# Row halves of the array: the low half of an expansion and a 1x1 convolution on 48 partitions, for two units at a time

## What is computed

```python
# L0: channel attention, then three convolutions
q, k, v = split(norm(x) @ w_qkv + b_qkv)
q2 = l2n((q - mean)**2 / sum, axis=channels); k2 = l2n((k - mean)**2 / sum, axis=tokens)
attn = (v + q2 @ (k2.T @ v) / 64) @ w_ln + b_ln
y = leaky(conv1x1(concat(attn, x), w1) + b1)      # 96 -> 96: "conv1"
y = leaky(conv3x3(y, w2) + b2)                    # 96 -> 96: "conv2"
x = conv1x1(y, w3) + b3 + x
# L1: relu, depthwise 3x3, 1x1, norm
# L2: weights mixed from 4 experts by a gate on the mean of the image
h = relu(norm(x @ Wk))                            # 48 -> 192: "expansion"
h = relu(norm(depthwise3x3(h)))
x = norm(h @ Wk2) + x
# L3: as L1
```

## Time and profile before

| | |
|---|---|
| median of 3 runs | 1022.58 us |
| the profiled execution | 1021.38 us, its span 1019.5 us |
| TensorE (PE) | 961.8 us busy, 94% of the span |
| VectorE (DVE) | 861.8 us, 85% |
| ScalarE (ACT) | 483.4 us, 47% |
| GpSimd (POOL) | 78.2 us, 8% |
| mean granted TensorE clock | 0.98 of full speed |
| start of conv2 in iterations 3, 4, 5 | 388.7, 504.8, 620.8 us: 116.1 us each |

### The profile page before, as it was taken

The page is one execution under the profiler, slowest core; times in us unless marked ns, Lnnn a source line. Parts: engine busy times, 40 slices in busy tenths (PEclk is TensorE's granted clock), DMA queues, the critical chain, the costliest instruction groups (busy, mean ns, idle before and its releaser), DMA issues.

```text
span 1019.5 us, 15287 instructions
## 1 busy us (share of the span) xinstructions
PE 961.8 (94%) x4854; PEld 611.8 (60%) x4854; DVE 861.8 (85%) x1229; ACT 483.4 (47%) x827; POOL 78.2 (8%) x112
## 2 busy tenths in 40 slices
PE   4799989999999999999999999999999999997987
PEld 4455756566665675666665675666666576554624
DVE  5773689997899969998799969999699978997980
ACT  3311554264724655365724655355733746344532
POOL 0210021000300012000300002000300003000000
PEclk8799989999999999999999999999999999998999
DMA  5243733385517654186516655177425665145315
GB/s 79 49 125 73 132 83 98 61 141 124 137 47 120 129 126 122 33 134 155 131 48 106 134 122 140 27 126 163 114 72 91 131 130 139 38 93 127 63 34 104
DMA packets 129520, 104.49 MB, mean 102 GB/s; under 512 B 97903, under 2 KB 98772, under 8 KB 129492
## 3 DMA queue, kind: packets, MB, share of 16 engines
q1 hardware_dynamic: 122196, 102.76, 48.4%
q10 hardware_dynamic: 7296, 1.38, 1.0%
HBM read 10.82 MB, written 6.29 MB: 17 GB/s over the span
## 4 chain that ended last, share of the span: by engine, by line
PE 69%; DVE 15%; ACT 5%; SPq 5%; issue 4%; DMA 2%; ACTq 1%; DVEq 0%
PE bank L1329 27%; PE bank L1365 7%; PE bank L1309 5%; PE bank L1335 5%; DVE dwa L717 4%; PE bank L1433 3%; SPq L1031 3%; PE bank L1380 3%; PE bank L1349 3%; PE bank L1381 3%; PE bank L1299 2%; DVE dwa L733 2%; DMA y_parts<-a_parts 2%; PE bank L1368 2%; PE bank L1367 2%
## 5 line engine op out<-in xcount | busy, mean ns | idle before, releaser
L717 DVE SCALAR_TENSOR_TENSOR dwa<-h1a,dyn,dwa 128x1024 f32<-128x1024 f32 x224 | 279.9, 1274 | 3.7 <-ACT dwa L1615 3.0
L1329 PE MATMUL bank<-y_parts,w_l 128*96 128x512 f32 x576 | 149.6, 404 | 0.6 <-issue 0.3
L1329 PE MATMUL bank<-y_parts,w_h 128*96 128x512 f32 x576 | 147.6, 400 | 0.0
L717 DVE SCALAR_TENSOR_TENSOR dwb<-h1b,dyn,dwb 128x1024 f32<-128x1024 f32 x112 | 142.8, 1275 | 0.0
L1177 POOL TENSOR_TENSOR y_low<-y,y_parts 96x512 fp32r<-96x512 f32 x56 | 73.7, 1316 | 774.9 <-DVE y L771 774.9
L1329 PEld LDWEIGHTS bank<-y_parts,w_l 128*96 128x96 f32 x576 | 90.8, 162 | 61.5 <-issue 22.4
L1365 PE MATMUL bank<-a_parts,wt_h 128*112 128x512 f32 x384 | 116.3, 410 | 6.8 <-DMA y_parts<-a_parts 6.0
L1329 PEld LDWEIGHTS bank<-y_parts,w_h 128*96 128x96 f32 x576 | 92.9, 161 | 44.3
L1365 PEld LDWEIGHTS bank<-a_parts,wt_h 128*112 128x112 f32 x384 | 62.7, 174 | 42.8 <-issue 21.1
L1309 PE MATMUL bank<-xq,w_cur 97*96 97x512 f32 x128 | 67.9, 611 | 3.5 <-DVE y L771 3.5
L1650 ACT ACTIVATE y<-bank,b2s 96x512 f32<-96x512 f32 x32 | 21.9, 683 | 102.6 <-PE bank L1335 102.6
(11 more groups left out here) (265 smaller groups left out, 1621.9 us busy)
## 6 DMA issues: line engine op xcount, KB each, us to landing
y_parts<-y_parts SPq DMA_DIRECT2D x32, 396.0 KB, 3.5
y_parts<-a_parts SPq DMA_DIRECT2D x64, 198.0 KB, 3.0
y_parts<-a_parts SPq DMA_DIRECT2D x64, 197.6 KB, 3.5
y_parts<-y_low SPq DMA_DIRECT2D x64, 132.0 KB, 3.3
a_parts<-a_parts SPq DMA_DIRECT2D x128, 66.0 KB, 2.4
tok<-in_x_dram SPq DMA_DIRECT2D x42, 192.0 KB, 5.0
x_even<-y_parts SPq DMA_DIRECT2D x32, 198.0 KB, 3.6
x_odd<-y_parts SPq DMA_DIRECT2D x32, 198.0 KB, 4.0
```

Of the source, the lines that this page charges most:

```text
L717: nc.vector.scalar_tensor_tensor(out=dst, in0=tap_input(n, t), scalar=weight, in1=dst, op0=ALU.mult, op1=ALU.add).then_inc(tap_step, 1)
L1329: nc.tensor.matmul(bank[0:C2, :], wgt[:, t, :], y1_parts[:, part, rows, cols], start=part + t == 0, stop=False)
```

## The change

**Expansion.** `expand_pair(f, n)` does an even and an odd unit together. `x2[par]` now lies on 112 partitions with zeros between: for even rows the high part on 0 to 47 and the low part on 64 to 111, for odd rows the other way about. The weights are on both halves (`wpw`, `ew_h`, `ew_l` on 112 partitions). The high weights still multiply all of it; the low weights multiply the 48 partitions of the high part alone, which for even units are the upper half and for odd units the lower half of the array's rows. Both banks of `ring_b` are taken at the start of a pair.

**conv1.** The queries have a tile of their own, `q2`, with both parities side by side, so four transposes serve two units. `conv1_pair` multiplies the queries (`w1_q`, 48 rows) and x (`w1_x`, 49 rows with the one) in two matmuls for each unit, even on one row half and odd on the other; x is read from `xcm`, as `transpose_x` left it. The results go to banks 4 to 7 in turn, two at a time. The attention's small matmuls write their result for both halves.

**Loads.** `load_xt` reads both parities into `q2` (4 DMAs), `load_x` both into `tok` (4 DMAs): 8 for an image. `load_x` now stands after `beside_l1(2, 3)` on SP's queue.

```diff
-        expand_beside = {7: (), 8: (9, 10, 11), **{k: (k + 2,) for k in range(7)}}
+        expand_beside = ((2, 3), (4, 5), (6, 7), (8, 9), (10, 11))
...
             def conv1(image, f):
-                for k in range(CHUNKS + 1):
-                    if image is not None and k < CHUNKS:
-                        if k == 0:
+                for j in range(PCHUNKS + 1):
+                    units = expand_beside[j] if f is not None else ()
+                    if j < PCHUNKS:
+                        if j == 0:
                             pe.wait_ge(q_scaled, image + 1)
-                        par, i0 = k % 2, 4 * (k // 2)
-                        bank = ring_a.take(pe, image, A_XQ + k)
+                        bank = ring_a.take(pe, image, A_XQ + j)
                         for m in range(4):
-                            last = nc.tensor.transpose(bank[0:C2, m * 128:(m + 1) * 128],
-                                                       token(par, i0 + m, Q_AT, C2), ident[:, :])
+                            last = nc.tensor.transpose(bank[0:P2, m * 128:(m + 1) * 128], q2[:, 4 * j + m, :], ident[:, :])
                         last.then_inc(xqt_done, 1)
...
+                    if j < PCHUNKS:
+                        for n in units[:1]:
+                            expand_pair(f, n)
+                    if j > 0:
+                        conv1_pair(image, f, j - 1)
+                    if j == PCHUNKS:
+                        for n in units[:1]:
+                            expand_pair(f, n)
+
+            def conv1_pair(image, f, j):
+                if j == 0:
+                    pe.wait_ge(w1_ready, image + 1)
...
+                else:
+                    pe.wait_ge(y1_max, CHUNKS * image + 2 * (j - 1))
+                pe.wait_ge(xq_ready, PCHUNKS * image + j + 1)
+                pixels = slice(j * BANK, (j + 1) * BANK)
+                for par, at in enumerate((0, ODD_AT)):
+                    nc.tensor.matmul(conv1_bank(2 * j + par)[0:C2, :], w1_q[at:at + C, :], xq[at:at + C, j % 2, :],
+                                     start=True, stop=False)
+                for par, at in enumerate((0, ODD_AT)):
+                    nc.tensor.matmul(conv1_bank(2 * j + par)[0:C2, :], w1_x[at:at + C + 1, :], xcm[at:at + C + 1, pixels],
+                                     start=False, stop=True).then_inc(conv1_done, 1)
...
+            def expand_pair(image, n):
+                pair = [ring_b.take(pe, image, B_E + n + par) for par in range(2)]
+                g = (n if n < 4 else n - 4) // 2
+                parts = [(at, slice(r * ROWS, (r + 1) * ROWS))
+                         for at, r in (((E_OTHER, g), (E_BOTTOM, g + 2)) if n < 4 else ((0, g),))]
+                for nth, (at, rows) in enumerate(parts):
+                    for par in range(2):
+                        nc.tensor.matmul(pair[par][:, :], ew_h[:, at:at + M1], x2[par][:, rows, 1:W + 1], start=nth == 0, stop=False)
+                for nth, (at, rows) in enumerate(parts):
+                    for par in range(2):
+                        own = slice(par * ODD_AT, par * ODD_AT + C)
+                        last = nc.tensor.matmul(pair[par][:, :], ew_l[own, at:at + M1], x2[par][own, rows, 1:W + 1],
+                                                start=False, stop=nth == len(parts) - 1)
+                        if nth == len(parts) - 1:
+                            last.then_inc(expand_done, 1)
...
             def iteration(f, attn, back):
                 beside_l1(sp, f, (0, 1))
                 if attn is not None:
+                    load_xt(sp, attn)
+                beside_l1(sp, f, (2, 3))
+                if attn is not None:
                     load_x(sp, attn)
-                beside_l1(sp, f, (2, 3))
```

More of the change, by code:

```diff
@@ L1221, in _ @@
             nc.tensor.matmul(banks[5][0:SUMS, 0:C2], p1[:, :], w1a[:, :], start=True, stop=True).then_inc(prep_pe, 1)
[L1222 to L1223 removed]
+            for at in (0, ODD_AT):
+                rows = banks[6][at:at + C + 1, 0:C2]
+                nc.tensor.matmul(rows, p1b[:, C:C2 + 1], w1a[:, :], start=True, stop=False)
+                last = nc.tensor.matmul(rows, ident[0:C2 + 1, C:C2 + 1], w1b[:, :], start=False, stop=True)
+            last.then_inc(prep_pe, 1)
             pe.wait_ge(prep_dve, marks["attention"])
@@ L1311, in conv1 @@
-                    for n in expand_beside[k] if f is not None else ():
-                        expand(f, n)
+                    if j < PCHUNKS:
[9 more added lines that the diff above has]
+                    pe.wait_ge(w1_ready, image + 1)
+                    for par in range(2):
+                        ring_c.take(pe, image, C_1 + par)
+                    if f is not None:
+                        after(pe, outc_ready, PCHUNKS * f)
+                elif j == 1:
+                    if f is not None:
+                        after(pe, ot_ready, 4 * f)
+                else:
[8 more added lines that the diff above has]
+                                     start=False, stop=True).then_inc(conv1_done, 1)
@@ L1466, in iteration @@
                         rows, cols = slice(0, (M1, M2)[n]), slice(n * M1, (M1, M)[n])
-                        nc.tensor.matmul(banks[7][0:C2, 192 + cols.start:192 + cols.stop], ones[rows, 0:C2], norm1[rows, cols],
+                        nc.tensor.matmul(banks[7][0:P2, 192 + cols.start:192 + cols.stop], ones[rows, 0:P2], norm1[rows, cols],
                                          start=True, stop=True).then_inc(prep_pe, 1)
@@ L1548, in _ @@
         def _(act):
+            load_xt(act, 0)
             load_x(act, 0)
@@ L1594, in conv1_slope @@
                         first_tap(f, 0)
-                    if image is not None and k > 0:
+                    for n in units if j < PCHUNKS else ():
+                        if n >= 4:
+                            h1a_rows(f, n)
+                    for k in (2 * j - 1, 2 * j) if j > 0 else ():
                         act.wait_ge(conv1_done, CHUNKS * image + k)
-                        if k == CHUNKS and f is not None:
-                            h1a_rows(f, expand_beside[k][0])
                         if k > Y1_BUFFERS:
```

205 lines of the change are left out of this document (107 added, 98 removed).

## The result

The change makes the kernel slower: median of 4 runs 1076.74 us (1069.93 to 1080.98) against 1022.75 us before, a ratio of 1.0522 with a 95% interval of 1.0495 to 1.0548. The profiled execution took 1073.48 us, its span 1071.6 us. I had predicted 1040 us and a range of 1023 to 1051: the sign was right, the size was not, and the result lies outside the range.

The account below looks back on a forecast made before the run. PE and DVE were taken as level bounds; 1021.4 us plus 15.4 (seven stretches of 2.2), 2.6 (start loads), -2.0 (conv1 of image 0) and 2.8 (last iteration) gave 1040 us, range 1023 to 1051.

Parts of the forecast that it names:

- block later than before: Each stretch of expansion and conv1: VectorE's depthwise block begins at 625.45 instead of 622.89 us, 2.6 us later.
- wait of VectorE that goes: VectorE's 0.4 us wait for conv2 disappears since PE is early, leaving 2.2 us lost per stretch.
- the last low part 0.6: VectorE's last low part of conv1, just ahead of the depthwise block, was taken to need 0.6 us.
- PE and DVE are level: From conv1's end to 578 us both engines bind; the 116.1 us iteration shortens only if conv2 and depthwise block begin earlier.
- rival 1: Faster: PE's saved work counts, 7 x 1.64 = 11.5 us go, giving 1008 us (996 by the skill's table); chance 0.13.
- prices of the row halves: On PE, 512 columns: fp32r pair 0.24 us, fp32 pair 0.86, overlapping; a visit costs 0.16 going in, 0.18 coming out.
- Rival 3: Much slower: row-half pairs don't overlap, each half takes its own 0.86 us, 5.1 us a stretch, 1076 us; chance 0.04.
- Rival 2: No change: unseen VectorE slack takes up the later depthwise block, PE's gain pays the ends, 1021 to 1025 us; chance 0.08.
- Sum. 1021.4 + 15.4 + 2.6 - 2.0 + 2.8: Profiled execution before, plus seven stretches, start loads, conv1 of image 0 and last iteration: 1040.2 us.
- Two more loads on ScalarE's queue, 2 x 1.3: At the start, two extra loads ahead of the chain's table load delay it by 2.6 us.
- -2.0 for conv1 of image 0: At the start, conv1 with four banks instead of two goes at VectorE's pace, less a later first result: 2.0 us saved.
- The last iteration: From the halo on, expansion pairs delay VectorE, the chain from there to the end: 942.95 instead of 940.16 us, +2.8.

Follow-up runs that it names:

- e_low: e_single with VectorE making the low parts of conv1's units 6 and 7, not of unit 7 alone: 1039.1 us, ratio 1.016.
- e_single: The changed kernel with expansion units one after another, each with its own bank and low weights on the full array; conv1 stays in row halves: 1041.0 us, ratio 1.019.
- e_own: e_single with each expansion unit's low matmuls alone on its own row half: 1064.6 us, ratio 1.042 to the kernel before.
- e_fill: The changed kernel with idle matmuls, results unread, in three of PE's gaps per iteration (two ahead of expansion pairs, one in conv2): 1059.1 us, ratio 1.036.
- b_exp: The kernel before with only the expansion in pairs, low weights on row halves; conv1, its transposes and loads unchanged: 1059.2 us, ratio 1.037.
- e_fill_all: e_fill plus idle matmuls in the start and the four loads into tok issued behind ScalarE's first square root: 1049.5 us, ratio 1.025.
- b_fill: The kernel before with idle matmuls of 128 columns in PE's gaps of the start, nothing else touched: 1016.6 us, ratio 0.993.
- e_pairfull: The changed kernel, both banks still taken at once, with the expansion's low weights on the full array instead of row halves: 1066.9 us, ratio 1.043.

## Why the prediction was wrong

**The stretch, step by step.** The steps held almost everywhere:

| step | predicted | measured |
|---|---|---|
| start of the first to the second pair | 3.73 | 3.81 |
| second to third pair | 3.34 | 3.40 |
| third pair to the end of conv1's third pair | 9.01 | 9.16 |
| from there to VectorE's first unit | 0.82 | 0.90 |
| that unit to the depthwise block | 6.89 | 7.56 |
| block later than before | 2.6 | 3.5 |
| wait of VectorE that goes | 0.4 | 0.5 |
| per iteration at full clock | 2.2 | 3.05 |

The term of the stretch that was mis-sized is the last low part: I wrote "the last low part 0.6", it took 1.46 from its start to the block's, since it waits for GpSimd, whose last low parts now come as VectorE wants to make its own. The units and the tap before it were 0.19 shorter than foreseen, so 0.67 of the 0.85 us by which an iteration was missed are this, and 7 x 0.85 = 6 us in all. e_low shows that VectorE waited for GpSimd; it does not show that the whole 0.86 reaches the iteration, since there VectorE pays 0.69 for the other unit. Two readings of the prediction were incomplete, with next to no weight in the sum: VectorE waits twice, not once, for 0.4 us in the window of the earlier trace rows, the second time for ScalarE's first tap just ahead of the block, and 0.2 + 0.59 us are 0.79, not 0.82.

**The argument "PE and DVE are level" was right**, and with it the rejection of rival 1: e_single's PE is 2.1 us earlier at conv2 and gains nothing by it. The prices of the row halves were right too (0.24 and 0.86 for a pair that overlaps; 0.34 for a visit, 0.38 measured in e_own). Rival 3 named 1076 us, the number that came out, but that is chance: its mechanism, pairs one after another, is refuted by the records 0.01 us apart. Rival 2 falls with iterations of 119.1 us.

**What failed: "Sum. 1021.4 + 15.4 + 2.6 - 2.0 + 2.8".** It has no term for TensorE's clock. I found idle times of 1.5 and 1.1 us ahead of the pairs and used them only as delays; in iterations 2 to 6 of the kernel before PE has no idle time of 0.5 us, and its few stretches at half clock lie at the start, in iteration 0 and in the last. With that idle time the rest of the stretch runs at half clock now and then, in this execution in iterations 5 and 6, 15.8 us for the two where 6.1 are the full-clock loss. e_fill, which fills the gaps, is worth 17.6 us, of which up to 3.4 are not its own. The gaps do not bring a fall each time: iterations 1 to 4 of the same execution have them and no fall, and so have b_exp (one of 1.33 us) and e_own (1.2 us in conv2) in all of the iterations 1 to 6. The four runs of the change spread over 11 us, the runs of the kernel before over 3, 5 and 9 us in the three groups, which fits it but shows nothing by itself.

In the terms of the sum, the profiled execution is 33.3 us above 1040.2: 16.9 in the seven iterations (32.3 for 15.4: 6 of the 16.9 are missed at full clock, 9.7 are the half clock of iterations 5 and 6), 8.8 in the start and 7.6 in the last iteration.

**The start**, predicted +0.6, was +9.4. "Two more loads on ScalarE's queue, 2 x 1.3": the table load came 5.3 us later, not 2.6, for the time that an issue takes is not constant (0.79 to 3.43 us for the four of L1039). The -2.0 for conv1 of image 0 was right at full clock and was lost to the clock: from its first matmul to the first conv2 e_fill_all takes 9.8 us and b_fill 12.4, both at full clock, -2.6; the change takes 15.2 and the kernel before 13.3, at mean granted clocks of 0.57 and 0.90. **The last iteration**, predicted +2.8, was +10.4; in e_fill, where its mean granted clock is 0.96 as before and not 0.92, it is +4.8. e_pairfull takes 172.1 us for it and e_single 165.2, a difference of 6.9, of which at most 4 are the clock (0.98 and 0.99), so the pairs are part of its cost too.

By parts, then: some 21 us are 7 x 3.05 of pairing, conv1's twos and GpSimd; 5 the loads of the start; about 5 the last iteration's pairs; the rest, some 20, I put down to the clock. The first three are read from the traces; the rest is what is left over, of which e_fill shows 14 to 18. How much of the clock's part belongs to the start and how much to each gap was not separated; the profiled executions differ there from each other.

Left open: why conv1 in row halves costs 0.95 us an iteration beside single units, and nothing beside pairs. Its results come in twos and VectorE still has four units to do when the third pair is done, which fits, but no run took that alone away.

## What to carry to other kernels

Before two units are joined to save matmuls, ask when their buffers are taken and when both results are there: joining moved the first wait earlier and the last result later, and cost 2.9 us where the saved matmuls gave 0.75. Where a prediction finds new idle time on TensorE, it needs a term for the clock as well as for the delay, and idle time of a kernel that is already there may be worth filling with matmuls that nobody reads: b_fill won 6 us by it. Compare by two marks on different engines rather than by whole iterations: here it placed the loss in one stretch at once.

## What the hardware showed that I had not expected

- Matmuls whose result is not used made two kernels faster: 17.6 us of 1076.7 (up to 3.4 of them by chance), and 6 us of 1022.6.
- Changing between the full array and row halves costs some 0.19 us each way with fp32r matmuls of 512 columns, whether the half is used by one matmul or two.
- One subtraction of 96 x 512 on VectorE takes 0.69 us where GpSimd is done, and 1.54 us where it is at work on a subtraction of its own.
- Issuing a load of one shape (L1039) took ScalarE's queue 0.79, 1.52, 1.60 and 3.43 us, one after another.
